# Products without a reader in the recurrence: nine behind the outputs and eight ahead of the carrier, in place of four and four

## The chip, the core and the metric

The kernel runs on one core of a Trainium2 chip. The time is the device time of one execution in microseconds (us); the time of a version is the median of its runs. The engines are TensorE (PE in the profile; its weight loads are PEld), VectorE (DVE), ScalarE (ACT), GpSimd (POOL) and SyncE (SP, which issues the transfers here).

## What is computed

The program is a model of two layers. The change lies in its first part, a recurrence over T = 2048 tokens of B = 2 sequences, with D = 256 channels and N = 16 complex states for each channel. Cut to what matters, a step is:

```python
def step(h, inp):
    x_t, dt_t, B_t, C_t, xr_t = inp
    h_carrier = h.mean(axis=1)
    T = jnp.cos((c_phase(xr_t) - c_phase(h_carrier)) / 2.0) ** 2
    alpha = jnp.exp(dt_t[..., None] * A_neg)
    expo = 1.0 + (1.0 - alpha) * KAPPA * (1.0 - T[:, None, :])
    mag, ph = (c_mag(h), c_phase(h))
    cmag = jnp.minimum(jnp.exp(expo * jnp.log(mag + 1e-08)), 10.0)
    h = from_polar(cmag, ph)
    h = h + B_t[:, None, :, :] * (dt_t * x_t)[:, :, None, None]
    h = from_polar(jnp.tanh(c_mag(h)), c_phase(h))
    y_t = jnp.einsum('bnc,bdnc->bd', C_t, h)
    return (h, y_t)
```

Each step needs the state of the step before, and the mean of that state over the channels (the carrier) enters the exponent. Slot attention, a scanner mixing, a long convolution, attention and ternary feed-forward layers follow; the change doesn't touch them.

## The kernel before, in words

The state fills 128 partitions with 64 elements for each of two components. The recurrence (`scan_phase`, L413) is a chain of small instructions. VectorE makes c, w, their squares, r2 and n2 (L740 to L753, by the helpers at L674 and L677), ScalarE takes logarithms and exponentials of them (l, M, ln2, E, rsq, L1, R, th2 by the helper at L595), VectorE makes the new state hb with its sums over the channels hs (L767), TensorE makes the carrier from hs (`carrier`, L532, matmuls at L536), ScalarE squares the carrier (L604) and works through lm, lnn, lnh, rs, ru and cm, and VectorE through Vm, dot, dl, s and V. With cm and V the next step begins.

Tokens are taken in 64 chunks of CS = 32 steps. The buffers of the chunks alternate (`par`), SyncE loads the next chunk's inputs while one is worked on, and the hardware loop's body has eight chunks, so it is run eight times. Each engine's order is written out by hand: `counts` has one semaphore per engine and parity, `DVE_STEP`, `ACT_STEP` and `PE_STEP` (L407 to L409) name the instructions that raise it in a step, and `after(engine, who, name, par, k)` waits until `who` has finished `name` of step k. All engines' orders are strict.

TensorE's step k (L563 to L581) is: wait for h1; the carrier (four matmuls in the code, eight in the trace, as float32 is issued in parts); `epsilon`, which puts a constant into the other carrier bank (L541); the four output matmuls into p_y (L570, eight in the trace); and then, in all steps of a chunk but the last, products that nothing reads. `keep_busy(slot, count)` (L545) issues `count` bfloat16 matmuls of a constant tile `warm`, 128 x 128 by 128 x 448, into columns 64 to 511 of the step's carrier bank, of which only columns 0 to 2 are used. Four of them stand behind the outputs and wait for dot (VectorE's read of this step's carrier), three wait for r2 of the next step, and one for E of the next step. Behind them, in TensorE's order, comes the next step's carrier.

Of the kernel before, what the change touches and what calls it, by code (L numbers as in the profile page):

```python
# [412 lines left out]
def scan_phase(nc, env):  # L413
# [19 lines left out]
    TAB_STEP = 2  # L433
    SHIFT = 2.0 ** 10
    FINAL = {who: CS * len(order) for who, (order, _) in STEPS.items()}
    CLEARS = len(STEPS)
    LEAVERS = len(STEPS)
    with Phase(nc, "scan") as ph:
# [14 lines left out]
        r2, dl = (state_ps[:, q * J:(q + 1) * J] for q in range(2))  # L453
# [4 lines left out]
        dot, s_, rs = (ph.sb(n, [P, 1]) for n in ("dot", "s", "rs"))  # L458
# [10 lines left out]
        def after(engine, who, name, par, k):  # L469

            if k < 0:
                par, k = 1 - par, CS - 1
            engine.wait_ge(counts[par][who], k * len(STEPS[who][0]) + STEPS[who][0].index(name) + 1)

        def before_step_0(engine, who):

            order, first = STEPS[who]
            engine.sem_inc(counts[1][who], FINAL[who] - (len(order) - order.index(first)))

        def leave(engine, k):  # L480

            if k == 1:
                engine.sem_inc(left, 1)
# [5 lines left out]
        with nc.Block() as block:  # L489
            @block.sync  # L490
            def _(sp):
                sp.dma_start(y_mask[:, :], ins["c_y_mask"]).then_inc(const, 16)
                sp.dma_start(mean_mat[:, :], ins["c_mean"]).then_inc(const, 16)
                sp.dma_start(h_start[:, :], ins["c_h_start"]).then_inc(const, 16)
                a_src = ins["L0_attn_a_A_log"].unsqueeze(1).to_broadcast([N, E])
                for b in range(B):
                    sp.dma_start(a_log[b * N * E:(b + 1) * N * E, :], a_src).then_inc(const, 16)

                def load(par, t0):
                    for b in range(B):  # L500
                        for e in range(E):
                            src = scratch[b, bass.ds(t0, CS), e * 2 * J:(e + 1) * 2 * J].unsqueeze(0).to_broadcast([N, CS, 2 * J])
                            dst = step_in[b * N * E + e:(b + 1) * N * E:E, par, :, :, :].rearrange("p t f j -> p t (f j)")
                            sp.dma_start(dst, src).then_inc(dma_in[par], 16)

                load(0, 0)
                sp.sem_inc(cleared, CLEARS)
                with sp.Fori(0, NCH // CHUNKS) as i:
                    for q in range(CHUNKS):
                        par, n = q % 2, i * CHUNKS + q  # L510
                        for who in STEPS:
                            sp.wait_ge(counts[1 - par][who], FINAL[who])
                        sp.wait_ge(left, (n + 1) * LEAVERS)
                        sp.sem_inc(taken, 1)
                        for who in STEPS:
                            sp.sem_clear(counts[1 - par][who]).then_inc(cleared, 1)
                        load(1 - par, (n + 1) * CS)
                sp.wait_ge(dma_in[0], (NCH // 2 + 1) * DMAS * 16)
                sp.wait_ge(dma_in[1], (NCH // 2) * DMAS * 16)
# [7 lines left out]
            @block.tensor  # L527
            def _(pe):
                pe.wait_ge(const, 16 * 5)
                pe.wait_ge(start, 3)  # L530

                def carrier(par, slot):  # L532

                    for q in range(4):
                        rows = slice(32 * q, 32 * q + 32)
                        last = nc.tensor.matmul(p_car[slot][rows, 0:2], mean_mat[rows, :], hs[rows, :], start=False, stop=True)  # L536
                    last.then_inc(counts[par]["pe"], 1)

                def epsilon(slot, start=True):

                    nc.tensor.matmul(p_car[slot][:, 0:3], env["ones"][0:1, :], eps_row[:, :], start=start, stop=not start)  # L541

                pe.wait_ge(warmed, 1)

                def keep_busy(slot, count):  # L545

                    for _ in range(count):
                        nc.tensor.matmul(p_car[slot][:, 64:512], warm[:, 0:P], warm[:, 64:512], start=True, stop=True)  # L548

                epsilon(1)  # L550
                before_step_0(pe, "pe")
                after(pe, "dve", "h1", 1, CS - 1)
                carrier(1, 1)
                after(pe, "pe", "carrier", 1, CS - 1)
                pe.sem_inc(counts[1]["pe"], 1)
                epsilon(0)
                with pe.Fori(0, NCH // CHUNKS) as i:
                    for q in range(CHUNKS):
                        par, n = q % 2, i * CHUNKS + q
                        pe.wait_ge(cleared, (n + 1) * CLEARS)  # L560
                        pe.wait_ge(mask_in, (n + 1) * MASKS)
                        pe.sem_inc(taken, 1)
                        for k in range(CS):  # L563
                            slot = k % 2
                            after(pe, "dve", "h1", par, k)
                            carrier(par, slot)
                            epsilon(1 - slot)
                            for half in range(2):
                                for comp in range(2):
                                    last = nc.tensor.matmul(p_y[par][J * half:J * half + J, k * 4:k * 4 + 4],  # L570
                                                            hb[:, slot, 2 - comp, :], c_masked[:, par, k, comp, 4 * half:4 * half + 4],
                                                            start=(comp == 0), stop=(comp == 1))
                            last.then_inc(counts[par]["pe"], 1)
                            leave(pe, k)
                            if k < CS - 1:
                                after(pe, "dve", "dot", par, k)
                                keep_busy(slot, 4)
                                after(pe, "dve", "r2", par, k + 1)
                                keep_busy(slot, 3)
                                after(pe, "act", "E", par, k + 1)  # L580
                                keep_busy(slot, 1)  # L581
                epsilon(0, start=False)

            @block.scalar
# [2276 lines left out]
```

## Time and profile before

| | |
|---|---|
| median of 3 runs | 12692.01 us (12689.93 to 12693.14) |
| the profiled execution | 12694.92 us |
| its span, first to last instruction | 12693.1 us |
| busy: TensorE, VectorE, ScalarE | 84%, 80%, 66% |
| products of L548 | 15,872 in 5455.5 us |
| recurrence | 262 to 9431 us |
| mean granted clock of TensorE | 0.75 of full speed |

The profile is of one execution. Busy is the time in which an engine had an instruction under way; matmuls overlap each other, and their ends are modelled. The granted clock is TensorE's clock as a share of full speed, 2.4 GHz; the records know two levels here, 0.50 (1.2 GHz) and 1.00, so a mean in between is a mixture in time. Idle time is put down to what ended it.

### The profile page before, as it was taken

What the parts mean: (1) busy time and instruction counts of PE and PEld (TensorE: products, weight loads), DVE (VectorE), ACT (ScalarE), POOL (GpSimd) and SP (SyncE); (2) the same over time, 40 slices, a digit from 0 to 9 for tenths busy, and PEclk for the clock granted to TensorE, in tenths of its full rate; (3) what the DMA queues carried; (4) which work ended last, traced back from release to release, by engine and by line L of the source; (5) the groups of instructions that cost most, each with busy time, mean ns of one, the idle gap of its engine ahead of it and who ended that gap; (6) DMA issues with size and microseconds to landing.
All of it is one profiled execution on the core that took longest, in us unless ns stands there. A gap on an engine that the chain in (4) does not pass through costs nothing. (4 is left out here: it accounts for less than half of the span.)

```text
span 12693.1 us, 256258 instructions
## 1 busy us (share of the span) xinstructions
PE 10620.3 (84%) x68398; PEld 5374.3 (42%) x68414; DVE 10121.4 (80%) x56587; ACT 8430.5 (66%) x42451; POOL 95.0 (1%) x165
## 2 busy tenths in 40 slices
PE   6888888888888888888888888888887978898998
PEld 5333333333333333333333333333344546653335
DVE  5888888888888888888888888888874948868875
ACT  6777777777777777777777777777764722264666
POOL 0000000000000000000000000000000100000000
PEclk8666667666666666666666666666678978998999
DMA  1000100001000100001000010001000000011100
GB/s 57 15 15 15 21 15 15 15 17 20 15 15 15 21 15 15 15 15 22 15 15 15 16 21 15 15 15 21 15 10 12 1 24 6 7 35 46 29 24 22
DMA packets 339618, 229.88 MB, mean 18 GB/s; under 512 B 27662, under 2 KB 324183, under 8 KB 337884
## 3 DMA queue, kind: packets, MB, share of 16 engines
q1 hardware_dynamic: 338140, 213.30, 7.9%
q8 instruction: 545, 8.93, 0.3%
q14 instruction: 933, 7.64, 0.2%
HBM read 187.41 MB, written 25.43 MB: 17 GB/s over the span
## 5 line engine op out<-in xcount | busy, mean ns | idle before, releaser
L548 PE MATMUL scan_p_car<-scan_warm 128*128 128x448 bf16 x15872 | 5455.5, 490 | 993.3 <-DVE scan_state_ps L674 985.4
L548 PEld LDWEIGHTS scan_p_car<-scan_warm 128*128 128x128 bf16 x15872 | 1513.7, 117 | 3681.5 <-DVE scan_state_ps L674 2094.0
L595 ACT ACTIVATE scan_act_ps<-scan_state_ps 128x64 f32<-128x64 f32 x2048 | 426.0, 208 | 1888.6 <-DVE scan_state_ps L674 1888.6
L595 ACT ACTIVATE scan_act_ps<-scan_act_ps 128x64 f32<-128x64 f32 (+1 forms) x8193 | 1611.6, 197 | 65.5
L536 PEld LDWEIGHTS scan_p_car<-scan_hs,scan_mean_mat 32*32 32x32 f32 x16392 | 372.2, 125 | 1846.5 <-DVE scan_hb L677 1834.2
L677 DVE SCALAR_TENSOR_TENSOR scan_uw<-scan_w,scan_rsq 128x64 f32<-128x64 f32 x2048 | 461.3, 225 | 854.2 <-ACT scan_rsq L595 854.2
L541 PE MATMUL scan_p_car<-scan_eps_row,ones 1*128 1x3 f32 x4102 | 1021.3, 316 | 39.1 <-DMA scan_a_log<-L_attn_a_A_log 38.9
L536 PE MATMUL scan_p_car<-scan_hs,scan_mean_mat 32*32 32x2 f32 x16392 | 548.5, 191 | 590.3 <-DVE scan_hb L677 568.0
L570 PE MATMUL scan_p_y<-scan_c_masked,scan_hb 128*64 128x4 f32 x16384 | 1037.8, 229 | 0.0
L674 DVE TENSOR_TENSOR scan_c<-scan_V,scan_power_ps 128x64 f32<-128x64 f32 x4096 | 724.6, 218 | 277.8 <-issue 47.6
L541 PEld LDWEIGHTS scan_p_car<-scan_eps_row,ones 1*128 1x128 f32 x4102 | 843.3, 255 | 72.0 <-DMA scan_a_log<-L_attn_a_A_log 39.3
L570 PEld LDWEIGHTS scan_p_y<-scan_c_masked,scan_hb 128*64 128x64 f32 x16384 | 858.6, 177 | 34.3
L595 ACT ACTIVATE scan_act_ps<-scan_norm_ps 128x64 f32<-128x64 f32 x4097 | 862.4, 211 | 0.0
L682 DVE TENSOR_SCALAR scan_bx<-scan_step_in,scan_tab 128x64 f32<-128x64 f32 x4098 | 843.7, 249 | 20.6 <-DMA scan_step_in<-scan_scratch 17.0
L677 DVE SCALAR_TENSOR_TENSOR scan_hb<-scan_R,scan_uw 128x64 f32<-128x64 f32 x4096 | 766.3, 224 | 26.3 <-ACT scan_th L595 2.6
L677 DVE SCALAR_TENSOR_TENSOR scan_Vm<-scan_mag,scan_hb 128x128 f32<-128x128 f32 x2049 | 597.6, 292 | 237.6 <-ACT scan_mag L595 5.5
L595 ACT ACTIVATE scan_power_ps<-scan_state_ps,scan_s 128x64 f32<-128x64 f32 x2049 | 590.8, 288 | 243.1 <-DVE scan_s L701 19.4
L2619 ACT ACTIVATE attn_pT<-attn_ps 128x1024 f32<-128x1024 f32 (+3 forms) x640 | 550.3, 896 | 280.4 <-PE attn_ps L2532 168.6
L674 DVE TENSOR_TENSOR scan_w<-scan_c,scan_bx 128x64 f32<-128x64 f32 x4096 | 727.6, 219 | 1.1
L674 DVE TENSOR_TENSOR scan_sq<-scan_w 128x64 f32<-128x64 f32 x4096 | 725.7, 219 | 0.0
L595 ACT ACTIVATE scan_alpha<-scan_step_in,scan_a_neg 128x64 f32<-128x64 f32 x2048 | 690.2, 337 | 18.8 <-issue 18.8
L674 DVE TENSOR_TENSOR scan_V<-scan_Vm,scan_ru 128x128 f32<-128x128 f32 x2049 | 597.4, 292 | 2.9
(453 smaller groups left out, 18358.4 us busy)
## 6 DMA issues: line engine op xcount, KB each, us to landing
scan_step_in<-scan_scratch SPq DMA_DIRECT2D x520, 256.0 KB, 6.2
qk_scratch<-qkv_parts SPq DMA_DIRECT2D x32, 384.0 KB, 2.5
attn_qT<-qk_scratch SPq DMA_DIRECT2D x192, 64.0 KB, 2.2
attn_kT<-qk_scratch SPq DMA_DIRECT2D x192, 64.0 KB, 2.2
scan_scratch<-prep_dts SPq DMA_DIRECT2D x32, 256.0 KB, 2.1
x<-L_attn_a_x SPq DMA_DIRECT2D x1, 4096.0 KB
out<-x SPq DMA_DIRECT2D x1, 4096.0 KB
filter_in_taps<-c_kT SPq DMA_DIRECT2D x1, 2048.0 KB
```

The lines of the kernel that those rows point to most:

```text
L536: last = nc.tensor.matmul(p_car[slot][rows, 0:2], mean_mat[rows, :], hs[rows, :], start=False, stop=True)
L541: nc.tensor.matmul(p_car[slot][:, 0:3], env["ones"][0:1, :], eps_row[:, :], start=start, stop=not start)
L548: nc.tensor.matmul(p_car[slot][:, 64:512], warm[:, 0:P], warm[:, 64:512], start=True, stop=True)
L570: last = nc.tensor.matmul(p_y[par][J * half:J * half + J, k * 4:k * 4 + 4], hb[:, slot, 2 - comp, :], c_masked[:, par, k, comp, 4 * half:4 ...
L595: nc.scalar.activation(dst, src, func, **kw).then_inc(counts[par]["act"], 1)
L674: nc.vector.tensor_tensor(out, a, b, op).then_inc(sem, 1)
L677: nc.vector.scalar_tensor_tensor(out, in0, scalar, in1, op0, op1, **kw).then_inc(sem, 1)
L682: nc.vector.tensor_scalar(bx[:, comp, :], step_in[:, par, k, 1, :], tab[:, par, k, comp:comp + 1], None, ALU.mult).then_inc(sem, 1)
L2619: nc.scalar.activation(pT[(2 * n + pair) % 4][:, :, off:], ps[:, 2 * pair:2 * pair + 2, off:], ACT.Exp).then_inc(exp_done, 1)
```

## The change

The group behind the outputs now stands in every step and has nine products; the group that waits for r2 of the next step has four, and the group that waits for E of the next step has four.

```diff
                             last.then_inc(counts[par]["pe"], 1)
                             leave(pe, k)
+                            after(pe, "dve", "dot", par, k)
+                            keep_busy(slot, 9)
                             if k < CS - 1:
-                                after(pe, "dve", "dot", par, k)
+                                after(pe, "dve", "r2", par, k + 1)
                                 keep_busy(slot, 4)
-                                after(pe, "dve", "r2", par, k + 1)
-                                keep_busy(slot, 3)
                                 after(pe, "act", "E", par, k + 1)
-                                keep_busy(slot, 1)
+                                keep_busy(slot, 4)
                 epsilon(0, start=False)
```

## Rows read from the trace of the kernel before

**Rows 1.** The page's slices, 40 equal ones: the granted clock in tenths.

```profile
PEclk8666667666666666666666666666678978998999
```

**Rows 2.** The waits: who waited for whom, us in total, times, longest us.

```profile
ACT scan_act_ps L595 <- DVE scan_state_ps L674: 1888.6, 2048, 4.2
DVE scan_uw L677 <- ACT scan_rsq L595: 854.2, 2048, 0.4
...
ACT scan_act_ps L595 <- PE scan_p_car L536: 13.3, 57, 0.3
```

**Rows 3.** Timeline of TensorE over three steps: start us, us, engine, line, operation.

```profile
4498.85 0.58 PE L548 MATMUL scan_p_car<-scan_warm 128*128 128x448 bf16 x1
4499.39 0.28 PE L536 MATMUL scan_p_car<-scan_hs,scan_mean_mat 32*32 32x2 f32 x8
...
4503.83 0.28 PE L536 MATMUL scan_p_car<-scan_hs,scan_mean_mat 32*32 32x2 f32 x8
...
4504.74 0.93 PE L548 MATMUL scan_p_car<-scan_warm 128*128 128x448 bf16 x4
4506.63 1.08 PE L548 MATMUL scan_p_car<-scan_warm 128*128 128x448 bf16 x4 [0.97 <-DVE scan_state_ps L674]
4507.35 0.10 PEld L548 LDWEIGHTS scan_p_car<-scan_warm 128*128 128x128 bf16 x1 [0.42 <-ACT scan_act_ps L595]
4508.27 0.24 PE L536 MATMUL scan_p_car<-scan_hs,scan_mean_mat 32*32 32x2 f32 x8 [0.55 <-DVE scan_hb L677]
...
4512.67 0.28 PE L536 MATMUL scan_p_car<-scan_hs,scan_mean_mat 32*32 32x2 f32 x8
```

**Rows 4.** Windows: busy us (instructions) by engine; then granted clock, DMA share, GB/s.

```profile
4499.40:4503.84 4.44, 4.44 (x29) 2.07 (x28) 3.73 (x26) 3.17 (x20) 0.00 (x0) 0.50 0.01 2
4504.20:4508.60 4.40, 2.88 (x28) 1.43 (x28) 3.73 (x25) 3.15 (x20) 0.00 (x0) 1.00 0.03 6
4511.00:4517.80 6.80, 6.77 (x40) 3.18 (x40) 5.55 (x39) 5.35 (x34) 0.00 (x0) 0.50 0.00 0
300.00:9431.00 9131.00, 7567.58 (x52528) 3571.75 (x52526) 7632.31 (x51245) 6628.97 (x39323) 0.00 (x0) 0.69 0.09 16
```

**Rows 5.** Timeline of ScalarE: its square of the carrier, two steps.

```profile
4504.18 0.16 ACT L595 ACTIVATE scan_act_ps<-scan_p_car 128x3 f32<-128x3 f32 x1
...
4508.57 0.16 ACT L595 ACTIVATE scan_act_ps<-scan_p_car 128x3 f32<-128x3 f32 x1
```

**Rows 6.** One line's instructions: ns min/median/max; and their mean by lines.

```profile
L536 PE MATMUL scan_p_car<-scan_hs,scan_mean_mat x16392: 166/188/210, 261.6 to 9430.5; 32*32 32x2 f32 x200
L548 PE MATMUL scan_p_car<-scan_warm x15872: 352/556/581, 267.8 to 9429.6; 128*128 128x448 bf16 x199
L536 PE MATMUL scan_p_car<-scan_hs,scan_mean_mat 32*32 32x2 f32 x16392 | 548.5, 191 | 590.3 <-DVE scan_hb L677 568.0
```

**Rows 7.** Timeline of TensorE at half clock: four products by themselves.

```profile
4500.65 1.68 PE L548 MATMUL scan_p_car<-scan_warm 128*128 128x448 bf16 x4
```

**Rows 8.** Timeline of TensorE from the last step of a chunk into the next.

```profile
4991.54 0.28 PE L536 MATMUL scan_p_car<-scan_hs,scan_mean_mat 32*32 32x2 f32 x8
...
4996.15 0.28 PE L536 MATMUL scan_p_car<-scan_hs,scan_mean_mat 32*32 32x2 f32 x8 [3.48 <-DVE scan_hb L677]
...
4997.41 3.22 PE L548 MATMUL scan_p_car<-scan_warm 128*128 128x448 bf16 x8
```

**Rows 9.** Timeline at a loop end: VectorE's and TensorE's first work.

```profile
4850.68 0.35 DVE L674 TENSOR_TENSOR scan_c<-scan_V,scan_power_ps 128x64 f32<-128x64 f32 x2 [6.05 <-issue]
4853.55 0.28 PE L536 MATMUL scan_p_car<-scan_hs,scan_mean_mat 32*32 32x2 f32 x8 [9.55 <-DVE scan_hb L677]
```

**Rows 10.** Timeline at the end of the recurrence.

```profile
9431.29 0.38 PE L541 MATMUL scan_p_car<-scan_eps_row,ones 1*128 1x3 f32 x2
...
9431.81 0.18 DVE L710 TENSOR_TENSOR xnT<-scan_p_y,rec_gate 128x32 f32 x1
9433.17 0.39 SPq L785 DMA_DIRECT2D yout_w_out<-L_attn_a_W_out  x1
```

## The prediction

> **What bounds the kernel now.** I read the page's slices first: for three quarters of the span the granted clock of TensorE stands at 6 tenths, slice by slice the same [rows 1]. That is the recurrence, from 262 to 9431 us. Then the waits: VectorE waits for ScalarE's rsq and ScalarE for VectorE's r2, each in all 2,048 steps [rows 2]. So the step is a ring through two engines, and TensorE enters it at one point, the carrier: L536 starts right after the second hb sum and ScalarE's square of it follows (L595, out of scan_p_car). Nothing on TensorE is in the ring beside the carrier; the products of L548 have no reader. They matter in two ways: they can stand in front of the carrier in TensorE's order, and they hold up the clock at which the carrier runs.
>
> The carriers of four steps in a row start at 4499.39, 4503.83, 4508.27 and 4512.67 us [rows 3]. The first two run at half clock (1.2 GHz), and the steps behind them take 4.44 us; the third runs at full clock (2.4 GHz) and its step takes 4.40 [rows 3, 4]. The eight carrier products take 0.28 us at half and 0.24 at full, and the square starts 0.35 us behind the first of them at half (4503.83 to 4504.18), 0.30 at full (4508.27 to 4508.57) [rows 3, 5]. **A step is thus worth 0.044 us more at half clock than at full**, which is all the clock buys; every other interval of the ring is VectorE's and ScalarE's and repeats to the hundredth. The clock over the whole recurrence is 0.69 [rows 4]. How many carriers meet the half clock: a carrier product lasts 188 ns in the middle, 191 in the mean, about 176 at full and 198 at half (166 and 187 are the first and last of eight at full, 187 and 210 at half) [rows 6]. (191-176)/(198-176) is 0.68; I take 1,390 of 2,048 steps.
>
> **The change, part by part.** It reorders nothing. In 31 of 32 steps the group behind the outputs grows from 4 to 9, the group ahead of the carrier from 3+1 to 4+4; in step 31 of a chunk nine stand where none stood. Per chunk 8 x 31 = 248 products become 17 x 31 + 9 = 536; in all 15,872 become 34,304, each a weight load and a matmul.
>
> *Do they fit at full clock?* Four in a row last 0.93 us, of which the last one's own 0.353 is partly pipeline; the spacing is 0.19 [rows 3, 6]. Nine take 1.72. The group begins at 4504.74 and r2 releases the next at 4506.63, so 1.89 us are there: 0.17 spare. Then eight take 1.53, from 4506.63, where the carrier is due at 4508.27: 1.64 us, 0.11 spare. The second four is released by E, which today's last product shows at 4507.35 [rows 3], 0.72 us behind 4506.63, when the first four have just gone. At half clock a carrier starts on time though the last product before it is shown to end later (4498.85 + 0.58 against 4499.39) [rows 3], so 0.11 is enough. Cost of the 17 at full clock: nothing, hidden under VectorE's c, w, sq, n2 and ScalarE's chain. If that cover goes, each product is 0.19 us in front of the carrier.
>
> *At half clock they do not fit.* The spacing is 0.373 ((1.68-0.58)/3 is 0.37) [rows 3, 7]. Seventeen take 6.34 us against the 3.53 between 4504.74 and 4508.27: the carrier would be 2.8 us late, and behind it square, lnn, rs, s and cm, one for one, since the square stands in ScalarE's order ahead of lm.
>
> *Does the clock hold?* Inside a chunk, yes. Now at full clock the products stream for 8 x 0.187 = 1.5 us of 4.40 and the clock falls again; at half clock 8 x 0.373 = 3.0 us of 4.44, and from there it rises [rows 3, 4]. After the change 17 x 0.187 = 3.2 us of 4.40 at full clock, more than stands before a rise now, and the longest stretch without a product is about 1.1 us (carrier, the epsilons, outputs). So the 1,390 steps lose 0.044 each: **-61 us**.
>
> *The boundary between chunks* is the weak place. Step 31 has no group ahead of the next carrier. Today TensorE idles 3.48 us there before the carrier of step 0 [rows 8]. With nine products behind the outputs of step 31, 1.7 us of this fill; from their end to the first product of step 0 (4.61 us behind the first of the nine, as today's carriers of these steps, 4991.54 and 4996.15 [rows 8]) 2.9 us remain with only carrier, epsilon and outputs. No row shows what the clock does over such a stretch between groups this dense: today's groups are too thin for it to stay full anyway. The bounds are no fall at all and a fall at all 64. Clock changes sit anywhere in the step [rows 4], so whether this stretch is caught is a matter of where it lies; I take half, plus the loop ends below: 33 falls.
>
> The price of one: the half clock falls onto the 17 products of step 0, which then run without a gap, so it should rise again within that step. Between 0 (back to full before them) and 2.8 us (half clock for all of them); the middle is 1.4, and at loop ends, where the clock is surely half as step 0 begins, I take 2.0. 26 x 1.4 + 7 x 2.0: **+50 us**.
>
> *Code and loop ends.* Every eighth chunk VectorE waits 6.05 us for nothing shown and TensorE idles 9.55 [rows 9]. TensorE now comes to that branch 1.7 (3.4 at half clock) us later; should it need the same 6.05, it is ready 1.8 us or even 0.1 us before its carrier. Cost 0; unhidden, 7 x 1.7 = 12. SP's and GpSimd's queues get nothing new.
>
> *The new wait for dot in step 31* queues nine products in front of the next carrier, which is due 3.5 us behind them: 1.7, or 3.4 at half clock, fit. In the very last step they start behind the last outputs, at about 9431.37 where the last epsilon (9431.29) ends today, and run 1.7 us to 9433.1; VectorE is done at 9431.99 (9431.81 + 0.18) and the next phase's first DMA goes at 9433.17 [rows 10]. The phase ends for all together: **+1.1**.
>
> Sum: -61 + 50 + 1 = -10. The profiled execution took 12694.9 us (span 12693.1), 2.9 over the median of 12692.0. 12694.9 - 10 = 12685; at the median's level **12,682 us**. A measurement of this kernel can tell about 0.2%, 25 us, from no change.
>
> **A rule against the row.** In the recurrence TensorE is busy 83% of the time, its idle stretches are about 1 us, and still the clock falls every few steps [rows 3, 4]. The Trainium skill, TensorE: Matmul & The Clock Gate, section "Why this matters for your kernels", says that long idle gaps between bursts are what sends the clock back to the lower level. By that rule alone the clock would be full today and the change worth nothing in the steps; the trace disagrees, so what streams counts and not only what is idle. At the new boundary trace and rule part again, which makes the first rival.
>
> **The rivals.** *No falls at boundaries.* The 2.9 us contain the carrier, epsilon and output matmuls; true idleness there is about 1.9 us (3.48 less 1.7, plus a little). If that is not enough for a fall, only the 7 loop ends cost: -61 + 7 x 2.0 + 1 = -46, or -60 without them. 12,632 to 12,646; I give 12,640. Against it: at full clock the clock falls today with gaps of 1 us. By the rule of the Trainium skill just named this is the outcome. Chance 0.2.
>
> *Falls at every boundary* (the slower side). Place: L577 of step 0, behind the outputs; price 1.4 to 2.8 each, 2.1 in the middle. 64 x 2.1 = 134, -61 + 134 + 1 = +74: 12,766; with 2.8 it is 12,811. It decides from a total of about 85 us of lateness: 60 falls at 1.4 or 31 at 2.8. For it: the stretch of 2.9 us is two thirds of a step, and thin ones fall readily now. Chance 0.22.
>
> *The clock doesn't hold inside chunks*, or 0.11 us of room isn't there. Were one carrier in ten late by 1.4, +287 us. Against it: 3.2 of 4.4 us streaming. Chance 0.05.
>
> **How the numbers follow.** My case has 0.53. Its own spread: 25 to 40 falls at 1.3 to 1.8 each are 32 to 72 us, so -28 to +12: 12,664 to 12,704. Of the 0.53, 0.44 are within 25 us of the median, 0.06 faster, 0.03 slower. With the rivals: faster 0.06 + 0.2 = 0.26, the same 0.44, slower 0.03 + 0.22 + 0.05 = 0.30. The range goes from the low end of the first rival, 12,632, to a little above the middle of the second, 12,780.
>
> **What would show it.** Granted clock of the recurrence at 0.95 or more, from 0.69; the mean of an L536 product at 176 to 180 ns, from 191; carriers 4.40 us apart inside chunks; L548 x34304; after about every second boundary one period 1.3 to 2.9 us too long, with ScalarE waiting for the carrier (13 us in 57 waits now [rows 2]) some 50 us in about 33. Wrong if that wait holds over 90 us, if falls come within chunks, or if carriers at full clock stand 4.44 us apart or more.

## The result, and the profile after

The changed kernel takes 12711.28 us (median of 20 runs, 12702.84 to 12716.71) where the kernel before takes 12692.15 (20 runs, 12686.81 to 12699.43). The ratio is 1.0015, with a 95% interval from 1.0008 to 1.0022: 19 us slower, small but beyond its noise. The profiled execution took 12702.84 us, the fastest of the 20, with a span of 12701.1, 8.0 us over the span before.

Of the page of the changed kernel, the first part's line of TensorE, the slices' clock, and two groups of the fifth part (busy us, mean ns, idle before):

```profile
PE 11872.6 (93%) x86830; PEld 6325.9 (50%) x86846; DVE 10058.4 (79%) x56587; ACT 8396.2 (66%) x42451; POOL 95.0 (1%) x165
...
PEclk8999999999999999999999999999998979998999
...
L548 PE MATMUL scan_p_car<-scan_warm 128*128 128x448 bf16 x34304 | 7268.6, 357 | 155.6 <-DVE scan_state_ps L674 28.5
...
L536 PE MATMUL scan_p_car<-scan_hs,scan_mean_mat 32*32 32x2 f32 x16392 | 489.1, 177 | 179.9 <-DVE scan_hb L677 166.7
```

The clock forecast came true: 9 tenths and more through the recurrence, from 6 [rows 1], and a carrier product at 177 ns in the mean, from 191 [rows 6]. TensorE now sits idle 180 us ahead of the carriers in all, from 590. Windows of the changed kernel (busy us by engine, then granted clock, DMA share, GB/s): one fall of the clock at a chunk's start, the 30 steps behind it, and the recurrence.

```profile
core 0: us, PE busy (x) PEld busy (x) DVE busy (x) ACT busy (x) POOL busy (x), PEclk, DMA share, GB/s
2993.30:2996.60 3.30, 3.30 (x11) 1.31 (x10) 2.74 (x20) 1.93 (x11) 0.00 (x0) 0.50 0.02 5
2996.80:3130.00 133.20, 130.77 (x1063) 66.99 (x1061) 111.08 (x752) 97.03 (x579) 0.00 (x0) 1.00 0.09 18
300.00:9431.00 9131.00, 8812.66 (x70851) 4519.28 (x70850) 7565.17 (x51219) 6591.05 (x39304) 0.00 (x0) 0.99 0.09 16
```

The last line answers to the 0.69 of [rows 4]. The waits show what came in exchange (us in total, times, longest):

```profile
ACT scan_act_ps L595 <- DVE scan_state_ps L674: 1873.4, 2048, 3.9
...
ACT scan_act_ps L595 <- PE scan_p_car L536: 93.1, 114, 3.0
```

ScalarE waits for the carrier 93.1 us in 114 waits, up to 3.0 us each, from 15.3 us in the whole trace before (13.3 in the stretch of [rows 2]), never over 0.3. Here is where it happens: TensorE's timeline from step 31 of one chunk to step 2 of the next.

```profile
2985.56 1.69 PE L548 MATMUL scan_p_car<-scan_warm 128*128 128x448 bf16 x8
2987.20 0.24 PE L536 MATMUL scan_p_car<-scan_hs,scan_mean_mat 32*32 32x2 f32 x8
...
2988.01 1.88 PE L548 MATMUL scan_p_car<-scan_warm 128*128 128x448 bf16 x9
2991.63 0.24 PE L536 MATMUL scan_p_car<-scan_hs,scan_mean_mat 32*32 32x2 f32 x8 [1.74 <-DVE scan_hb L677]
...
2992.45 5.07 PE L548 MATMUL scan_p_car<-scan_warm 128*128 128x448 bf16 x17
2997.45 0.24 PE L536 MATMUL scan_p_car<-scan_hs,scan_mean_mat 32*32 32x2 f32 x8
...
2998.27 3.63 PE L548 MATMUL scan_p_car<-scan_warm 128*128 128x448 bf16 x17
3001.84 0.24 PE L536 MATMUL scan_p_car<-scan_hs,scan_mean_mat 32*32 32x2 f32 x8
```

Step 31 ends with nine products at 2988.01, at full clock, 1.88 us. Then nothing streams until 2992.45. The carrier of step 0 stands on time at 2991.63, after 1.74 us of idleness. The 17 products of step 0 take 5.07 us where the 17 of step 1 take 3.63; the clock records have TensorE at half for 3.4 us from 2993.24 on, and full on both sides of it. The carrier of step 1 starts at 2997.45, 5.82 us behind the one before it; the next follows after 4.39. ScalarE's squares of the same two carriers:

```profile
2991.93 0.16 ACT L595 ACTIVATE scan_act_ps<-scan_p_car 128x3 f32<-128x3 f32 x1
...
2997.75 0.16 ACT L595 ACTIVATE scan_act_ps<-scan_p_car 128x3 f32<-128x3 f32 x1 [1.39 <-PE scan_p_car L536]
```

The 1.39 us of idleness before the second one is the price. All of it goes into the ring: the step takes 5.82 us in place of 4.40.

**Where the time went.** I take the recurrence from the first to the last hb sum, and as lateness of a carrier the distance of its first product from the hb sum less the 0.056 us that it has when it is on time, added over all steps. Both are worked out from the records of every step.

| | recurrence, us | late carriers | lateness, us | recurrence less lateness | span outside it |
|---|---|---|---|---|---|
| before | 9164.0 | 0 | 0 | 9164.0 | 3529.1 |
| changed | 9171.0 | 50 | 81.0 | 9090.0 | 3530.1 |
| changed, second profile (e9 below) | 9180.6 | 56 | 85.3 | 9095.3 | 3537.3 |

So the clock gives back 74 us (69 in the second profile), and late carriers take 81 (85). All 50 and all 56 late carriers belong to step 1 of a chunk; no carrier is late in any other step. Of the 50, 42 stand behind the 56 boundaries inside the loop's body (60.5 us), seven behind the loop ends and one behind the start (20.5 us together); in the second profile 48 (67.9 us) and eight (17.5 us).

### The profile page after: what moved, and what is told of

It is laid out like the page before. It is cut to its first block and busy times, and to the rows that moved or that the text cites. A ratio compares the mean times of both kernels' runs of the same rounds, so it can differ in the third digit from the quotient of the medians.

```text
span 12701.1 us, 293122 instructions
## 1 busy us (share of the span) xinstructions
PE 11872.6 (93%) x86830; PEld 6325.9 (50%) x86846; DVE 10058.4 (79%) x56587; ACT 8396.2 (66%) x42451; POOL 95.0 (1%) x165
## 5 line engine op out<-in xcount | busy, mean ns | idle before, releaser
L548 PE MATMUL scan_p_car<-scan_warm 128*128 128x448 bf16 x34304 | 7268.6, 357 | 155.6 <-DVE scan_state_ps L674 28.5
L548 PEld LDWEIGHTS scan_p_car<-scan_warm 128*128 128x128 bf16 x34304 | 2968.0, 98 | 3599.3 <-DVE scan_state_ps L674 993.3
L570 PE MATMUL scan_p_y<-scan_c_masked,scan_hb 128*64 128x4 f32 x16384 | 839.2, 205 | 0.0
L541 PE MATMUL scan_p_car<-scan_eps_row,ones 1*128 1x3 f32 x4102 | 780.7, 258 | 39.1 <-DMA scan_a_log<-L_attn_a_A_log 38.9
L536 PEld LDWEIGHTS scan_p_car<-scan_hs,scan_mean_mat 32*32 32x32 f32 x16392 | 312.6, 103 | 982.5 <-DVE scan_hb L677 950.7
L570 PEld LDWEIGHTS scan_p_y<-scan_c_masked,scan_hb 128*64 128x64 f32 x16384 | 659.7, 137 | 34.5
L536 PE MATMUL scan_p_car<-scan_hs,scan_mean_mat 32*32 32x2 f32 x16392 | 489.1, 177 | 179.9 <-DVE scan_hb L677 166.7
L541 PEld LDWEIGHTS scan_p_car<-scan_eps_row,ones 1*128 1x128 f32 x4102 | 602.0, 183 | 72.7 <-DMA scan_a_log<-L_attn_a_A_log 39.3
```

## The experiments

Theory A: between chunks there is a stretch without products, the clock falls there, and the half-clock products of step 0 make the carrier of step 1 late. Rival B: the time is the price of 18,432 more products, wherever they stand. Rivals C and D are narrower and stand in the expectations of e3 and e4. "Late" counts carriers more than 0.05 us late. Each ratio is to the kernel before, measured beside the edit.

**e1: the stretch is filled.** At the head of a chunk, with 9, 4 and 4 otherwise as in the changed kernel:

```diff
                         pe.sem_inc(taken, 1)
+                        after(pe, "dve", "r2", par, 0)
+                        keep_busy(1, 4)
+                        after(pe, "act", "E", par, 0)
+                        keep_busy(1, 4)
                         for k in range(CS):
```

> The boundary is filled: at the head of each chunk TensorE also issues four products at r2 and four at E of step 0, so that every step has 17. Theory A (the stretch without products between chunks lets the clock fall, and the half-clock products of step 0 make the carrier of step 1 late): late carriers fall from 50 to about 8 (the 7 loop ends and the start), their lateness from 81 us to about 20, the granted clock of the recurrence goes over 0.99, and the time to some 60 us under the changed kernel, 12,640 to 12,655. Rival B (the time is the price of the larger number of products, in order or in code, wherever they stand): 512 more products make it no faster than 12,711.

Measured: 12654.42 us (6 runs) against 12694.3, ratio 0.9968 [0.9956, 0.9980]. 9 late carriers with 13.0 us. The same place in TensorE's timeline (step 31, step 0, step 1):

```profile
2969.18 0.24 PE L536 MATMUL scan_p_car<-scan_hs,scan_mean_mat 32*32 32x2 f32 x8
...
2970.00 3.67 PE L548 MATMUL scan_p_car<-scan_warm 128*128 128x448 bf16 x17
2973.61 0.24 PE L536 MATMUL scan_p_car<-scan_hs,scan_mean_mat 32*32 32x2 f32 x8
...
2974.43 3.63 PE L548 MATMUL scan_p_car<-scan_warm 128*128 128x448 bf16 x17
2978.01 0.24 PE L536 MATMUL scan_p_car<-scan_hs,scan_mean_mat 32*32 32x2 f32 x8
```

17 products stand before each carrier, 3.67 and 3.63 us of them, both at full clock, and the carriers follow each other at 4.43 and 4.40. ScalarE's wait for the carrier (the helper's line is four further down here):

```profile
ACT scan_act_ps L599 <- PE scan_p_car L536: 26.8, 73, 1.7
```

With 512 products more than the changed kernel it is 57 us faster by the medians: the number is not the price. B falls.

**e2: the stretch is longer.** The nine of step 31 are left out.

```diff
-                            after(pe, "dve", "dot", par, k)
-                            keep_busy(slot, 9)
                             if k < CS - 1:
+                                after(pe, "dve", "dot", par, k)
+                                keep_busy(slot, 9)
```

> The changed kernel without the nine products of step 31; all other groups as in it. Theory A: the stretch without products grows from 2.9 to 4.6 us, all 63 boundaries and the start end with a late carrier in step 1, 1.4 us each and more where the clock is still low at the first product: 64 late carriers with 110 to 150 us, 12,740 to 12,780. Rival B: 576 products fewer, so the same as the changed kernel or some us less, 12,705 to 12,711.

Measured: 12756.47 us (4 runs) against 12694.3, ratio 1.0052 [1.0037, 1.0068]. 64 late carriers, each in step 1, 123.0 us; ScalarE's wait for the carrier:

```profile
ACT scan_act_ps L596 <- PE scan_p_car L536: 135.0, 129, 2.7
```

576 products fewer, 45 us slower than the changed kernel. This is what the larger groups would have cost without the group in step 31.

**e3: only the group of step 31.** The kernel before, with its 4, 3 and 1, and nine products in step 31:

```diff
                             leave(pe, k)
+                            after(pe, "dve", "dot", par, k)
+                            keep_busy(slot, 4 if k < CS - 1 else 9)
                             if k < CS - 1:
-                                after(pe, "dve", "dot", par, k)
-                                keep_busy(slot, 4)
```

> The kernel before with nine products behind the outputs of step 31 alone; groups of 4, 3 and 1 elsewhere. Theory A: eight products a step keep the clock where it was, 0.69 to 0.70, no carrier is late because eight at half clock fit; 12,688 to 12,693, no change. Rival C (the new wait for dot at the end of a chunk, or TensorE coming later to the next chunk, costs by itself): 20 us or more over before.

Measured: 12696.87 us (10 runs) against 12694.3, ratio 1.0003 [0.9993, 1.0012]. The granted clock is 0.70 and no carrier is over 0.06 us late. The window of its recurrence:

```profile
300.00:9431.00 9131.00, 7656.05 (x53114) 3595.28 (x53113) 7631.99 (x51259) 6626.58 (x39333) 0.00 (x0) 0.70 0.09 16
```

The new wait at the end of a chunk costs nothing that can be told: C's 20 us lie outside the interval, which ends at 15. C falls.

**e5: only the group behind the outputs grows.** 9, 3 and 1, and nine in step 31: 13 a step.

```diff
                                 after(pe, "dve", "r2", par, k + 1)
-                                keep_busy(slot, 4)
+                                keep_busy(slot, 3)
                                 after(pe, "act", "E", par, k + 1)
-                                keep_busy(slot, 4)
+                                keep_busy(slot, 1)
```

> Nine behind the outputs in every step as in the changed kernel, but three at r2 and one at E as before: 13 a step. Theory A: the clock holds inside chunks all the same (above 0.96), falls at boundaries stay as often (40 to 50) and the late carriers too, but at half clock 13 products need 4.85 us where 17 need 6.34, so each is late by about 0.65 us in place of 1.43 and the loop ends by 1.3: 30 to 37 us in place of 81. 12,660 to 12,670. Rival B: the product count falls by 7,936, so it lies between before and the changed kernel, 12,700.

Measured: 12675.76 us (11 runs) against 12694.3, ratio 0.9986 [0.9977, 0.9995]: faster than before. 53 late carriers, but of 42.0 us in all; 0.67 us is the typical one. 12 of them are not in step 1: with 13 products the clock sometimes falls inside a chunk too. Thirteen take 3.0 us at full clock with a gap before the carrier:

```profile
2991.17 3.02 PE L548 MATMUL scan_p_car<-scan_warm 128*128 128x448 bf16 x13
2994.75 0.24 PE L536 MATMUL scan_p_car<-scan_hs,scan_mean_mat 32*32 32x2 f32 x8 [0.55 <-DVE scan_hb L677]
```

The price of a fall is lower with four products ahead of the carrier than with eight, 0.67 us typically in place of 1.43, as A has it. The forecast of 12,660 to 12,670 was too low by 6 us; the 12 late carriers outside step 1, which A did not have, account for it.

**e9: the changed kernel again,** unedited.

> The changed kernel once more, for a second profile: the profiled execution was the fastest of 20 and had 49 falls of the clock and 50 late carriers. Theory A: an execution near the median (12,711) has more falls, up to all 64 boundaries, 55 to 64 late carriers with 88 to 105 us. If instead it has 50 and 81 us again, what lies between 12,703 and 12,711 is outside the late carriers.

Measured: 12716.75 us (11 runs) against 12695.9, ratio 1.0016 [1.0007, 1.0025]. Its profiled execution took 12719.71 us, 16.9 over the first one's: 4.3 of that are six more late carriers (56, 85.3 us), 5.3 the rest of the recurrence (a step at full clock takes 4.400 us here and 4.396 there), and 7.2 lie outside the recurrence, in code that the change doesn't touch. So executions differ by several us in every part. The expectation was 88 to 105 us of lateness; 85.3 is a little under it, and most of the 16.9 us lie outside the late carriers.

**e4: less to be late behind.** The groups at r2 and E are left out in step 0.

```diff
-                            if k < CS - 1:
+                            if 0 < k < CS - 1:
```

> The changed kernel with the groups at r2 and E left out in step 0 of each chunk, so nine products stand between the carriers of steps 0 and 1 in place of 17. Theory A: the clock falls at nearly every boundary (55 to 64), but nine at half clock need 3.36 us of the 3.53 there, so the carrier of step 1 is on time; where the half clock lasts into step 1, the carrier of step 2 is late. 40 to 72 us of lateness in place of 81, 12,670 to 12,700. Rival D (the late carriers come from something else at a chunk's start than the order behind half-clock products): step 1's carrier stays 1.4 us late.

Measured: 12708.17 us (10 runs) against 12695.9, ratio 1.0010 [1.0001, 1.0019]. 56 late carriers with 75.7 us, but 49 of them are now in step 2, 1.42 to 1.7 us mostly; those of step 1 are at most 0.29 late, and 7 are. The timeline of one chunk's first steps:

```profile
2846.39 0.24 PE L536 MATMUL scan_p_car<-scan_hs,scan_mean_mat 32*32 32x2 f32 x8 [1.74 <-DVE scan_hb L677]
...
2847.20 1.88 PE L548 MATMUL scan_p_car<-scan_warm 128*128 128x448 bf16 x9
2850.78 0.24 PE L536 MATMUL scan_p_car<-scan_hs,scan_mean_mat 32*32 32x2 f32 x8 [1.70 <-DVE scan_hb L677]
...
2851.60 5.07 PE L548 MATMUL scan_p_car<-scan_warm 128*128 128x448 bf16 x17
2856.60 0.24 PE L536 MATMUL scan_p_car<-scan_hs,scan_mean_mat 32*32 32x2 f32 x8
```

Step 0 has nine products, its idle time before the carrier of step 1 is 1.70 us, and that carrier (2850.78) is on time. But the lean step is a second stretch without products, the clock falls one step later, and the 17 of step 1 (5.07 us) delay the carrier of step 2 (2856.60). D falls: step 1's carrier is on time when fewer products stand before it. The forecast of 12,670 to 12,700 was a miss: the edit moved the cost where I had thought it would shrink.

**e6: only the groups ahead of the carrier grow.** 4, 4 and 4, none in step 31: 12 a step.

```diff
-                            after(pe, "dve", "dot", par, k)
-                            keep_busy(slot, 9)
                             if k < CS - 1:
+                                after(pe, "dve", "dot", par, k)
+                                keep_busy(slot, 4)
```

> Only the groups ahead of the carrier as in the changed kernel (four and four), four behind the outputs and none in step 31: 12 a step. Theory A: all 12 fit at full clock but not at half (4.48 us of 3.53); 12 at full clock stream 2.2 us of 4.40 with a stretch of about 2.2 us nearly empty around carrier and outputs, so the clock also falls inside chunks: hundreds of late carriers of up to 1.3 us, 400 to 1,300 us slower than before. If the number alone decided, it would lie between before and the changed kernel.

Measured once, so without an interval: 12766.82 us against 12695.9, 71 us slower. 112 late carriers with 130.7 us: 64 in step 1, 23 in step 2, 25 elsewhere. The window of its recurrence:

```profile
300.00:9431.00 9131.00, 6934.81 (x59979) 3533.82 (x59976) 7528.83 (x50870) 6549.90 (x39037) 0.00 (x0) 0.97 0.09 16
```

The direction was right, the size (400 to 1,300 us) far off: inside chunks the clock holds with 12 products as well, but for some 15 falls. Twelve products fit at full clock and give most of what 17 give (the recurrence less its lateness is 9100.4 us); what they lose, they lose mostly at the boundary. About half of the late carriers (54 of 112) are 1.46 us late, twice the 0.67 of e5, though this kernel has one product a step fewer: it has eight behind the wait for r2 where e5 has four. So it is the products there, and not the total, that set the price.

**e8: 13 products and no stretch.** e5 with three at r2 and one at E across the boundary, as in e1.

```diff
                         pe.sem_inc(taken, 1)
+                        after(pe, "dve", "r2", par, 0)
+                        keep_busy(1, 3)
+                        after(pe, "act", "E", par, 0)
+                        keep_busy(1, 1)
```

> Nine behind the outputs, three at r2 and one at E, the last two also across the chunk's end: 13 in every step. Theory A: the clock holds across boundaries nearly as with 17 (falls at the loop ends and at up to 20 others), a fall costs 0.7 us in place of 1.4: 10 to 20 us of lateness, 12,640 to 12,655, as with 17 and the ends filled or a little better.

Measured: 12671.91 us (11 runs) against 12695.9, ratio 0.9980 [0.9971, 0.9989]. 38 late carriers with 33.8 us. The boundaries are quiet (2 of the 38 stand there, 8 behind loop ends and the start), 28 fell inside chunks at 0.67 to 0.76 us each. A miss: filling the boundary gives 17 products 57 us; with 13 the medians of e5 and e8 are 4 us apart and their intervals overlap. With 13 the falls are cheaper and come elsewhere.

**e10: e1 again,** unedited.

> The filled boundary once more, for a second profile and an interval over more runs. Theory A: again about 9 late carriers with 12 to 18 us, all at the loop ends and the start; the recurrence 50 us or more shorter than before. The first time the kernel was only 40 us faster than before, with 14 us lost behind the recurrence, where nothing was changed; if that is the state of one execution the gain is now 45 to 55 us, if it comes with the code it stays 40.

Measured: 12651.95 us (5 runs) against 12696.95, ratio 0.9963 [0.9949, 0.9976]. 12 late carriers, 20.1 us; the span outside the recurrence is 3534.1 us where e1 had 3544.7, so the slow part behind e1's recurrence belonged to that execution and not to the code. The gain of 45 us is the low end of the forecast.

**e11: e1 with leaner loop ends.** In the first of the eight chunks of the loop's body no products at E before step 0, none ahead of step 1's carrier.

```diff
                         after(pe, "dve", "r2", par, 0)
                         keep_busy(1, 4)
-                        after(pe, "act", "E", par, 0)
-                        keep_busy(1, 4)
+                        if q:
+                            after(pe, "act", "E", par, 0)
+                            keep_busy(1, 4)
...
-                            if k < CS - 1:
+                            if k < CS - 1 and (k or q):
```

> The filled boundary, but in the first chunk of the loop's body (after each loop end, and at the start) the four at E before step 0 and the eight ahead of step 1's carrier are left out: at half clock four take 1.5 us of the 1.64 and nine 3.36 of the 3.53, so neither carrier is late. Theory A: the 13 us of lateness of the filled boundary fall to between 0 and 11, the latter where the clock is still half in step 1 or falls behind it; 2 to 13 us under the filled boundary in the same round.

Measured: 12654.16 us (5 runs) against 12696.95, ratio 0.9966 [0.9952, 0.9979]; 14 late carriers with 13.1 us: 8 of at most 0.29 us in step 1, but 6 of 1.6 to 2.2 us in step 2, behind which 17 products still met the half clock. No gain over the filled boundary (12,652 measured beside it, e10); the same lesson as e4.

**e12: half a bridge.** e1 without the four at E before step 0.

```diff
                         after(pe, "dve", "r2", par, 0)
                         keep_busy(1, 4)
-                        after(pe, "act", "E", par, 0)
-                        keep_busy(1, 4)
```

> The boundary filled by half: four products at r2 of step 0, none at E. The stretch without products before the first product of step 0 shrinks from 2.9 to about 1.9 us. Theory A: full clock holds over it at most boundaries as it does over the 1.1 us inside a chunk: 8 to 20 late carriers with 15 to 35 us, 12,640 to 12,670. Rival: any step with fewer than 17 products is enough for a fall: 50 or more late carriers, 12,711.

Measured: 12649.80 us (5 runs) against 12696.95, ratio 0.9963 [0.9950, 0.9976]. 8 late carriers, 17.1 us, all in step 1 behind the seven loop ends and the start. An ordinary boundary, and below it a loop end:

```profile
2969.05 0.24 PE L536 MATMUL scan_p_car<-scan_hs,scan_mean_mat 32*32 32x2 f32 x8
...
2969.87 2.92 PE L548 MATMUL scan_p_car<-scan_warm 128*128 128x448 bf16 x13
2973.49 0.24 PE L536 MATMUL scan_p_car<-scan_hs,scan_mean_mat 32*32 32x2 f32 x8 [0.70 <-DVE scan_hb L679]
...
2974.31 3.63 PE L548 MATMUL scan_p_car<-scan_warm 128*128 128x448 bf16 x17
2977.89 0.24 PE L536 MATMUL scan_p_car<-scan_hs,scan_mean_mat 32*32 32x2 f32 x8
```

```profile
2545.32 1.67 PE L548 MATMUL scan_p_car<-scan_warm 128*128 128x448 bf16 x4 [5.51 <-DVE scan_state_ps L676]
2546.95 0.28 PE L536 MATMUL scan_p_car<-scan_hs,scan_mean_mat 32*32 32x2 f32 x8
...
2548.22 5.31 PE L548 MATMUL scan_p_car<-scan_warm 128*128 128x448 bf16 x17
2553.45 0.24 PE L536 MATMUL scan_p_car<-scan_hs,scan_mean_mat 32*32 32x2 f32 x8
```

In the first, TensorE is idle 0.70 us before the carrier of step 0 and the clock holds, as it does at all 56 boundaries inside the loop's body: a step with 13 products is harmless between steps with 17, and the rival of its expectation falls. The four products both shorten the stretch and add to what streams in it, so this run doesn't tell which of the two counts. In the second VectorE's stall has left the clock at half; the four at r2 fit (1.67 us, carrier on time), the 17 behind take 5.31, and the next carrier is 2.0 us late. **e12 and e1 beat both kernels**; measured beside the kernel before for the last time (e10 and e12), each took 0.37% less.

## Why the prediction was wrong

The forecast was 12,682, no change or a little faster; the kernel is 19 us slower. The range of 12,632 to 12,780 holds that; the direction does not fit. The mechanism was the right one, and **the term that failed is the number of falls at boundaries**, 26 ordinary ones taken, 42 and 48 measured. The loop ends and the start add to it.

- *What a step buys at full clock*, 0.044 us, and the ring itself: right. The carriers inside chunks are 4.396 us apart, from 4.441 at half.
- *The gain of 61 us*: too small, 74 and 69 were measured. Carriers whose eight products last over 185 ns in the mean, and so met the half clock, are 1,399 before and 9 now; 1,390 times 0.044 is the 61 us. About 8 us more came from a place I had no term for, below, and 3 from the steps at loop ends.
- *17 products fit at full clock*: right. No carrier outside step 1 is late, in 1,984 steps. By the timeline nine take 1.88 us, of the 1.89 that are there; the 0.17 us said to be spare there is the last product's own length, and its absence did no harm.
- *The clock holds inside chunks*: right for 17, and e5, e8 and e6 show that 13 and 12 hold it with exceptions.
- *The price of a fall*, 1.4 us and 2.0 at loop ends: right for the first, 1.30 to 1.43 us (and one of 2.90), low for the loop ends and the start, 1.4 to 3.0 us, 2.6 in the mean of the first profile and 2.2 in that of the second. The start of the recurrence, which is late too (2.14 us), had no term.
- *The number*: "I take half, plus the loop ends: 33 falls." There were 49 falls and 50 late carriers in one profile, 55 and 56 in the other. 81.0 us in place of 50: of the 31 us more, 24 are the 16 ordinary boundaries above the 26 and 7 the loop ends and the start. Half was a choice for want of a row, on the thought that a fall is a matter of where the stretch lies. The stretch of 2.9 us was caught at 42 of 56 ordinary boundaries, and at 48 in the second profile. The falls are not scattered evenly: in both traces late carriers stand in two to nine chunks in a row, with one chunk spared behind each row, and in the second, from chunk 10 on, the spared chunks come again 16 chunks later. Why, no run here tests.
- *The loop ends and the code*: nothing extra, right; e3 shows the wait for dot in step 31 at no cost. *The end of the phase*: +1.1 forecast. In the changed kernel the last nine products run from 9439.26 to 9441.14; VectorE ends at 9439.96 and the next phase's first DMA is issued 2.63 us later, from 1.18 [rows 10]: +1.45.

```profile
9439.26 1.88 PE L548 MATMUL scan_p_car<-scan_warm 128*128 128x448 bf16 x9
...
9439.78 0.18 DVE L710 TENSOR_TENSOR xnT<-scan_p_y,rec_gate 128x32 f32 x1
...
9442.59 0.39 SPq L785 DMA_DIRECT2D yout_w_out<-L_attn_a_W_out  x1
```

The sum with what was measured: -74 + 81 in the recurrence and +1 outside it, which holds the 1.5, is the +8 between the two profiled executions. With the second profile it is -69 + 85 in the recurrence and +8 outside it; unrounded, 24.8 us, as the spans have it. The medians, 19 us apart, lie between.

*The rivals.* "Falls at every boundary" had the sign, with 12,766 it was too high by the price (2.1 taken, 1.62 and 1.52 measured per late carrier) and by a quarter of the boundaries in the first profile, an eighth in the second. The recorded chance was 0.22, and the kernel came out between my case and this rival. e2 is the kernel in which it holds in full, 12,756. "No falls" was wrong by itself, and it is what e1 and e12 make true: 12,650 to 12,654, for which 12,640 was worked out. The rule of the Trainium skill (TensorE: Matmul & The Clock Gate, "Why this matters for your kernels") leaned to that rival. The traces don't bear it out at the ordinary boundaries: with 1.7 to 2.1 us of idleness before the carrier of step 0 the clock fell at 42 and 48 of 56, and in e12 with 0.70 to 0.85 us at none. At the loop ends, where TensorE idles 6.8 to 7.6 us before that carrier, it fell at all seven in both profiles, as the rule has it.

## What to carry to other kernels

Work that only keeps the clock up and doesn't fit before the critical instruction at the lower clock becomes, at each fall, the delay it was meant to avoid; the more of it stands between the last wait and that instruction, the dearer each fall (e5 against e6). Look for the stretches that the filler does not cover, chunk and loop boundaries first, and cover them before making the groups larger: here four products at the head of a chunk were worth 60 us, and without them the larger groups lost 19. Thinning the step behind such a stretch only moved the delay one step on (e4, e11).

## What the runs showed that I had not expected

- The clock has a second path into the ring, at the end of a chunk. VectorE reads the outputs of step 31 (L710) before it begins the next step. One boundary of the kernel before, at half clock, and below it one of the changed kernel, at full:

```profile
2841.22 0.60 PE L570 MATMUL scan_p_y<-scan_c_masked,scan_hb 128*64 128x4 f32 x8
2841.75 0.29 ACT L595 ACTIVATE scan_power_ps<-scan_state_ps,scan_s 128x64 f32<-128x64 f32 x1
2842.00 0.19 DVE L710 TENSOR_TENSOR xnT<-scan_p_y,rec_gate 128x32 f32 x1
2842.31 0.35 DVE L674 TENSOR_TENSOR scan_c<-scan_V,scan_power_ps 128x64 f32<-128x64 f32 x2
```

```profile
2845.18 0.41 PE L570 MATMUL scan_p_y<-scan_c_masked,scan_hb 128*64 128x4 f32 x8
2845.91 0.29 ACT L595 ACTIVATE scan_power_ps<-scan_state_ps,scan_s 128x64 f32<-128x64 f32 x1
2846.04 0.18 DVE L710 TENSOR_TENSOR xnT<-scan_p_y,rec_gate 128x32 f32 x1
2846.27 0.35 DVE L674 TENSOR_TENSOR scan_c<-scan_V,scan_power_ps 128x64 f32<-128x64 f32 x2
```

At half clock the outputs end late, and from the start of ScalarE's cm (its line in each fence) to VectorE's next c pass 0.56 us in place of 0.36. In the kernel before, 38 of the 56 ordinary boundaries are 0.2 us longer in this way, in the changed kernel none. (Eight of the 56, one in each run of the loop's body, have 0.36 us more in both kernels; I have not looked for the reason.) Step 31 took 4.68 us in the middle and takes 4.43. This is read from the traces and was not tried by itself.
- With 12 products a step the granted clock of the recurrence was 0.97 (e6), with 13 0.99 (e5, e8), with 17 0.99 to 1.00, where eight left it at 0.69; the step from eight is larger than that from 13 to 17.
- A step at full clock took 4.400 us in one execution and 4.396 or 4.397 in the others, and parts that no edit touches differ by up to 17 us in their span (3528.1 to 3544.7). Differences under 10 us were taken from counts of late carriers and not from times.
